# Queries and keys turned by VectorE blocks and a trip through DRAM instead of on TensorE, with plain float32 scores

## What is computed

```python
# layer 0: q, k turned by position (rope); layers 1 and 3: q, k normalised by their rms, times a weight
q = (layernorm(x) @ Wq).reshape(B, S, 32, 128);  k = (ctx @ Wk).reshape(B, S, 8, 128);  v = (ctx @ Wv)...
scores = einsum('bhqd,bhkd->bhqk', q, repeat(k, 4)) / sqrt(128) + mask
attn = softmax(scores);  x = x + tanh(g) * (einsum('bhqk,bhkd->bhqd', attn, v) @ Wo)
```

## Time and profile before

| | us |
|---|---|
| median of 3 runs | 2615.45 (2614.41 to 2617.41) |
| span of the profiled execution | 2614.6 |
| PE busy | 2382.5 (91%) |
| DVE busy | 1786.3 (68%) |
| POOL busy | 1512.2 (58%) |
| ACT busy | 1278.9 (49%) |

### The profile page before, as it was taken

How to read it: one execution, slowest core, us unless ns; L and a number is a source line. 1 busy time by engine, 2 the same in 40 slices (tenths; PEclk the granted TensorE clock), 3 DMA queues, 4 the chain that set the end, 5 groups by cost and what they waited for, 6 DMA issues and landing times.

```text
span 2614.6 us, 41410 instructions
## 1 busy us (share of the span) xinstructions
PE 2382.5 (91%) x13005; PEld 2016.6 (77%) x13005; DVE 1786.3 (68%) x3406; ACT 1278.9 (49%) x3698; POOL 1512.2 (58%) x1567
## 2 busy tenths in 40 slices
PE   5899999998889999999887887899689999999977
PEld 4788888886778888888766776776578888888753
DVE  4677777777877777777666676563477777777752
ACT  2555555554246666666534455233245666665421
POOL 5666666665246666666535667423456666666543
PEclk9999999999999999999999999899889999999979
DMA  3234444443224233223310000259513233322344
GB/s 110 80 118 155 141 160 159 151 162 109 71 84 142 97 98 102 93 93 98 109 49 17 1 1 27 81 193 365 175 61 108 91 98 101 101 94 77 116 169 151
DMA packets 191532, 288.12 MB, mean 110 GB/s; under 512 B 15985, under 2 KB 110833, under 8 KB 188378
## 3 DMA queue, kind: packets, MB, share of 16 engines
q1 hardware_dynamic: 175584, 236.34, 27.1%
q0 software_dynamic: 10224, 42.03, 4.6%
q10 hardware_dynamic: 5514, 7.11, 0.9%
HBM read 218.80 MB, written 100.37 MB: 122 GB/s over the span
## 4 chain that ended last, share of the span: by engine, by line
PE 73%; DVE 8%; DMA 6%; POOL 5%; issue 4%; ACT 3%; SPq 0%; POOLq 0%; ACTq 0%; DVEq 0%
PE B_qkv L806 32%; PE B_out L806 19%; PE B_more L883 4%; PE B_s L863 4%; PE B_qT L852 3%; DMA slots_y<-S 3%; PE B_more L806 2%; PE B_s L864 1%; PE B_more L957 1%; DMA out_x<-rows_last 1%; PE B_s L806 1%; DVE xn L1523 1%; DVE X L1650 1%; PE B_qT L806 1%; PE B_more L855 1%
## 5 line engine op out<-in xcount | busy, mean ns | idle before, releaser
L1333 ACT ACTIVATE W<-S,nmx 128x128 f32<-128x128 f32 x768 | 298.1, 395 | 49.9 <-DVE nmx L1625 48.8
L2183 POOL TENSOR_TENSOR S<-S,mask 128x512 f32<-128x512 f32 x184 | 256.6, 1394 | 46.9 <-ACT S L1162 46.9
L1226 ACT ACTIVATE sq<-B_qkv 128x640 f32<-128x640 f32 x127 | 89.7, 706 | 380.1 <-PE B_qkv L806 380.1
L2228 POOL TENSOR_TENSOR pT_l<-W,pT_h 128x512 fp32r<-128x512 f32 x184 | 241.8, 1314 | 32.9 <-ACT pT_h L1162 30.7
L2157 POOL TENSOR_SCALAR rn<-ss 128x5 f32<-128x5 f32 x128 | 25.3, 198 | 371.3 <-DVE ss L1563 371.3
L806 PE MATMUL B_qkv<-ring_h,xnT_h 128*128 128x512 f32 x540 | 216.2, 400 | 11.3 <-DVE spare_l L1474 4.8
L2222 POOL TENSOR_TENSOR W<-W,rden 128x512 f32<-128x512 f32 x192 | 202.1, 1052 | 32.7 <-DVE rden L1630 32.6
L806 PE MATMUL B_qkv<-ring_l,xnT_h 128*128 128x512 f32 x540 | 214.5, 397 | 0.0
L806 PE MATMUL B_out<-ring_h,oT_h 128*128 128x512 f32 x516 | 206.1, 399 | 8.7 <-DVE kT L1615 4.4
L806 PE MATMUL B_qkv<-ring_h,xnT_l 128*128 128x512 f32 x540 | 212.8, 394 | 0.0
L863 PE MATMUL B_s<-kT,qT_h 128*128 128x256 f32 x768 | 191.1, 326 | 17.8 <-DVE xnT_l L1474 15.1
(11 more groups left out here) (514 smaller groups left out, 7730.5 us busy)
## 6 DMA issues: line engine op xcount, KB each, us to landing
raw<-in_pieces SPq DMA_DIRECT2D x270, 256.0 KB, 2.6
between_p<-S SPq DMA_DIRECT2D x184, 256.0 KB, 2.2
W<-between_p SPq DMA_DIRECT2D x184, 256.0 KB, 2.8
slots_x<-in_zero SPq DMA_DIRECT2D x32, 1030.0 KB, 6.0
raw<-in_experts SPq DMA_DIRECT2D x16, 768.0 KB, 6.5
w<-in_experts SPq DMA_DIRECT2D x8, 1024.0 KB, 14.0
slots_y<-S SPq DMA_DIRECT2D x31, 256.0 KB, 6.4
xn<-slots_x ACTq DMA_DIRECT2D x8, 257.5 KB, 5.8
```

The costliest lines, as they stand in the source:

```text
L1333: t = act.activation(W[:, k, cols(r)], S[:, k, cols(r)], ACT.Exp, bias=nmx[:, k, r:r + 1], accum_out=den[:, k, r:r + 1])
L2183: pool.tensor_tensor(S3, S3, m.unsqueeze(1).to_broadcast([P, R, P]), ALU.add).then_inc(*masked.now((layer, u)))
L2228: pool.tensor_tensor(heads_first(pT[1][:, :]), by_block(W[:, k, :]), heads_first(f32(pT[0][:, :])), ALU.subtract).then_inc(*p_split.now((l ...
```

## The change

For all units but those of TURNED_BY_PE, q and k are turned as the probabilities are. Per such unit:

- PE no longer turns q and k (5 products with the identity), ACT and DVE no longer split them in high and low parts.
- `blocks_q` (i+1, 19 in the norm layers, 22 in the rope layer): DVE turns the 32x32 blocks of `qk` into `sq`, 640 columns. `store_q` (i+1, 63) writes `sq` to DRAM (320 KB), `load_q` (i+1, 64) reads it back into `qkT` in rows by block; it waits for the store to have landed and for the queries of the unit before to have been copied. `copy_k` (i+2, 30): ACT copies the keys (with their weight) and then the four heads of queries from `qkT` to rows packed by head, `keys` and `queries`.
- `scores` (i+2, 40): one plain float32 product of 128 columns for each head, into the single bank `B_sc`.
- `low_scores` goes, on ACT and POOL. `mask` on DVE scales the scores and adds the mask in one instruction.
- `sq` is free again when `store_q` has landed (`sq_read`). What writes it next, ACT's squares in the norm layers and DVE's product with cos in the rope layer, waits for that.
- Units with odd u in the middle of a layer project into the two banks `B_turn`, which the turned q and k had, and the others into `B_qkv`.

The units of TURNED_BY_PE still turn q and k on PE, and have the plain float32 scores too.

```diff
-            self.at(i + 1, 50, "turn_q", layer, u)
-            self.at(i + 1, 50, "split_k", layer, u)
+            if (layer, u) in TURNED_BY_PE:
+                self.at(i + 1, 50, "turn_q", layer, u)
+                self.at(i + 1, 50, "copy_k", layer, u)
+            else:
+                self.at(i + 1, 19 if KINDS[layer] == "norm" else 22, "blocks_q", layer, u)
+                self.at(i + 1, 63, "store_q", layer, u)
+                self.at(i + 1, 64, "load_q", layer, u)
+                self.at(i + 2, 30, "copy_k", layer, u)
             self.at(i + 2, 40, "scores", layer, u)
-            self.at(i + 2, 41, "low_scores", layer, u)
...
+            if NB <= u < G * NB - NB and u % 2:
+                return B_turn, ("qT", "kT")
+            return B_qkv, ("qkv",)
...
+        def sq_read(layer, u):
+
+            if (layer, u) in TURNED_BY_PE:
+                return (summed if KINDS[layer] == "norm" else roped).of((layer, u))
+            return q_stored[unit(layer, u)[3]].of((layer, u))
...
                 for r in range(R):
-                    pe.matmul(B_s[:, cols(r, 2 * P)], qT[0][:, cols(r)], kT_both[:, :], start=True, stop=False)
-                    t = pe.matmul(B_s[:, cols(2 * r)], qT[1][:, cols(r)], kT[0], start=False, stop=True)
+                    t = pe.matmul(B_sc[:, cols(r)], query(r), keys[:, :], start=True, stop=True)
...
+                    act.wait_ge(*q_loaded[unit(layer, u)[3]].of((layer, u)))
+                    copy(keys_by_block, keys_in, scale).then_inc(*keys_made.now((layer, u)))
+                    copy(queries[:, :, :], qkT[:, :, 0:R].rearrange("p t r -> p r t")).then_inc(*q_copied.now((layer, u)))
...
                     if u:
+                        dve.wait_ge(*sq_read(layer, u - 1))
                         dve.wait_ge(*roped.of((layer, u - 1)))
...
+            def blocks_q(layer, u):
+
+                kind = KINDS[layer]
+                dve.wait_ge(*{"rope": roped, "norm": normed}[kind].of((layer, u)))
+                if kind == "norm":
+                    dve.wait_ge(*summed.of((layer, u)))
+                dve.transpose(sq_blocks, qk[:, :].rearrange("p (h j q) -> p h j q", j=BLOCKS, q=BLOCK)
+                              ).then_inc(*q_blocks.now((layer, u)))
...
+                dve.scalar_tensor_tensor(out=S3, in0=per_head(B_sc), scalar=SCALE, in1=m.unsqueeze(1).to_broadcast([P, R, P]),
+                                         op0=ALU.mult, op1=ALU.add).then_inc(*sc_read.now((layer, u)))
...
+            def store_q(layer, u):
+                k = unit(layer, u)[3]
+                sync.wait_ge(*q_blocks.of((layer, u)))
+                if q_loaded[k].made:
+                    sync.wait_ge(q_loaded[k].sem, q_loaded[k].by * q_loaded[k].made)
+                sync.dma_start(between_q[k].rearrange("(p n) -> p n", p=P), sq[:, :]).then_inc(*q_stored[k].now((layer, u)))
+
+            def load_q(layer, u):
+                k = unit(layer, u)[3]
+                sync.wait_ge(*q_stored[k].of((layer, u)))
+                if u and (layer, u - 1) not in TURNED_BY_PE:
+                    sync.wait_ge(*q_copied.of((layer, u - 1)))
```

More of the change, by code:

```diff
@@ L465, in build @@
         sq = sb("sq", [P, (R + 1) * P])
+        with ExitStack() as besides_small_heads:
+            qkT = besides_small_heads.enter_context(nc.sbuf_tensor("qkT", [P, P, R + 1], F32))
+            keys = besides_small_heads.enter_context(nc.sbuf_tensor("keys", [P, P], F32))
+            queries = besides_small_heads.enter_context(nc.sbuf_tensor("queries", [P, R, P], F32))
         qT = [sb(f"qT_{k}", [P, HG], F32R) for k in "hl"]
@@ L629, in build @@
                                 "pT_hi", "oT_hi"))
-        rows_hi, low_scored = signal("rows_hi"), signal("low_scored")
+        rows_hi, keys_made, q_copied, q_blocks = (signal(n) for n in ("rows_hi", "keys_made", "q_copied", "q_blocks"))
+        q_stored, q_loaded = ([signal(f"{n}{k}", 16) for k in range(2)] for n in ("q_stored", "q_loaded"))
         y_copied = {"act": signal("y_copied_act"), "dve": signal("y_copied_dve")}
@@ L1312, in scores @@
                 qT_reader[:] = [scored.of((layer, u))]
-            def low_scores(layer, u):
-                k = unit(layer, u)[3]
-                act.wait_ge(*scored.of((layer, u)))
-                if layer == 0 and u == 0:
-                    act.wait_ge(*const.of("mask0"))
-                if layer == 3 and u < 2:
-                    for t in range(TILES2 - 2, TILES2):
-                        act.wait_ge(*y_stored[t % 2].of((2, t)))
-                elif k in S_reader:
-                    act.wait_ge(*S_reader[k])
-                copy(per_head(S[:, k, :]), score_parts[:, :, 1, :], SCALE).then_inc(*low_scored.now((layer, u)))
             def exp(layer, u):
@@ L1472, in vector_program @@
         def vector_program(dve):
+            S_reader = {}
             def sub(dst, a, b):
@@ L1588, in normalise @@
                 if u or layer == 1:
-                    dve.wait_ge(*qk_turned.of((layer, u - 1) if u else (0, len(plan.units[0]) - 1)))
+                    dve.wait_ge(*(qk_read(layer, u - 1) if u else qk_read(0, len(plan.units[0]) - 1)))
                 else:
@@ L1618, in mask @@
-            def mask(layer, u):
-                k = unit(layer, u)[3]
+            def blocks_q(layer, u):
[5 more added lines that the diff above has]
+                              ).then_inc(*q_blocks.now((layer, u)))
+            def mask(layer, u):
+                kind, g, b, k, vs = unit(layer, u)
+                dve.wait_ge(*scored.of((layer, u)))
+                if layer == 0 and u == 0:
+                    dve.wait_ge(*const.of("mask0"))
+                if layer == 1 and u == 0:
+                    dve.wait_ge(*small["mask13"].of(0))
+                if layer == 3 and u < 2:
+                    for t in range(TILES2 - 2, TILES2):
+                        dve.wait_ge(*y_stored[t % 2].of((2, t)))
+                elif k in S_reader:
+                    dve.wait_ge(*S_reader[k])
+                m = mask0[:, b, :] if kind == "rope" else mask13[:, :]
@@ L1624, in mask @@
+                S_reader[k] = (exped if (layer, u) in TURNED_BY_PE else p_stored[k]).of((layer, u))
                 dve.wait_ge(*sc_read.of((layer, u)))
-                dve.tensor_reduce(nmx[:, k, :], S3, AX, ALU.max, negate=True).then_inc(*maxed.now((layer, u)))
+                dve.tensor_reduce(nmx[:, k, :], per_head(S[:, k, :]), AX, ALU.max, negate=True).then_inc(*maxed.now((layer, u)))
             def denominators(layer, u):
@@ L2373, in load_p @@
                                between_p[k].rearrange("(i p n) -> p i n", i=BLOCKS, p=P)).then_inc(*p_loaded[k].now((layer, u)))
+            def store_q(layer, u):
[9 more added lines that the diff above has]
+                    sync.wait_ge(*q_copied.of((layer, u - 1)))
+                elif layer == 1:
+                    sync.wait_ge(*q_copied.of((0, len(plan.units[0]) - 1)))
+                elif layer == 3:
+                    sync.wait_ge(*scored.of(CHUNKS - 1))
+                    sync.wait_ge(*kbd_made2.of(NB - 1))
+                sync.dma_start(qkT[:, :, :].rearrange("p (i q) h -> p i (q h)", i=BLOCKS), between_q[k].rearrange("(i p n) -> p i n", i=BLOCKS, p=P)
+                               ).then_inc(*q_loaded[k].now((layer, u)))
             def fill_tables():
@@ L2413, in sync_program @@
                     parts[name](*args)
-            for done in (*landed, *p_stored, *p_loaded, scales_in, cols_in, cleared, *consts2_in, dispatch_in, *y_stored, *scattered, *rows_in, *weight_in, *x_in, *small.values(), *rope_in):
+            for done in (*landed, *p_stored, *p_loaded, *q_stored, *q_loaded, scales_in, cols_in, cleared, *consts2_in, dispatch_in, *y_stored, *scattered, *rows_in, *weight_in, *x_in, *small.values(), *rope_in):
                 if done.made:
```

129 lines of the change are left out of this document (51 added, 78 removed).

## The result

The changed kernel takes **3440.14 us** (median of 4 runs, 3432.38 to 3448.66), against 2616.43 for the kernel before (4 runs): ratio **1.3138**, interval 1.3107 to 1.3169. It is slower by 824 us. The forecast was 3216 with a range of 2950 to 3450: the sign and the mechanism hold, the size was 224 us short, and the measured time lies only 10 us under the upper end.

The account below looks back on a forecast made before the run. PE bounds the kernel before; after the change the loop through sq and q's store was to bind. Norm layers 417, rope layer 83, clearing stores 54 and edges 47 give +601 on 2614.6: 3216 us, range 2950 to 3450.

Parts of the forecast that it names:

- What bounds before, and PE's part: PE alone sets the pace in the steady middles; its work falls from 9.05 to about 8.6 us a unit.
- ACT ahead of the scores: Scores wait for ACT's oT_h, keys and queries: PE stands still some 1.7 us a unit, giving 10.3 us.
- The rival of 2845: If the loop through sq is shorter than 10.3 us, only ACT's standstill remains: +230, 2845 us; chance 0.12.
- The norm loop: Norm layers, squares through p's store and q's store to next squares: 13.1 us against 9.05; 103 x 4.05 = 417.
- PE fits in, with 2.9 us to spare: Norm layers: scores and projections end at 10.2 us, 2.9 before squares may start, so PE is not in the loop.
- The rope layer: DVE's product with cos writes sq and waits for q's store: 10.7 us a unit, 50 x 1.65 = 83.
- PE falls back in: Waits lower PE's clock; if over 2.9 us is lost, a norm unit costs about 1 us more: 3320; chance 0.16.
- The clearing stores: q's store stands behind a clearing store in the queue: +1.7 us in 32 steps, 54 us.
- The edges: 31 units at the edges of the layers, priced by no row: 1.5 us each taken, 47 us.
- the sum of 601: Norm layers 417, rope layer 83, clearing stores 54 and edges 47, added to the profiled 2614.6 us.

Follow-up runs that it names:

- Experiment 8: Against the kernel before: q and k of all units turned on PE, no DRAM trip, but plain float32 scores and DVE's mask; 2583.93 us, ratio 0.9867.
- Experiment 1: Changed kernel with q's store issued right behind DVE's turn of its blocks, ahead of the probabilities' load and its wait; 3065.79 us, ratio 1.1712.
- experiment 4: Changed kernel with q's store and load moved ahead of SP's wait for p's store, and key and query copies ahead of oT_h; 2833.29 us.
- experiment 2: Changed kernel with ACT's squares written to another buffer in units 8 to 39 of layer 1, so they need not wait for q's store; 3405.14 us.

## Why the prediction was right, and where its size was off

- **What bounds before, and PE's part.** Right. The turn of q is PE's only saving; the scores took 0.89 us where 0.92 was taken. Experiment 8's row gives 0.89 us, 0.02 more than the float32r products had. By the four passes of true float32 (the Trainium skill, FP8 and Floating Point Precision, TensorE Precision Notes) PE would have kept less of its 0.48 us; no cost of that kind shows in this row.
- **ACT ahead of the scores.** The order was right, two prices were not: queries took 1.12 us, not 0.60, keys 0.47 to 0.56, not 0.36. Experiment 1 shows the step by itself: PE stands still 2.15 us where 1.7 was worked out, and the unit is 10.93 us where 10.3 was. What the step left out is the clock: 19 of the 44 units ran below the full one, at 12.68 us. The rival of 2845 says this with the lower prices, and its nearest kernel is that of experiment 1 (3066). That experiment 4 came to 2833 does not bear it out, since there the copies stand first.
- **The norm loop.** Right in every link. The two turns from 1501.20 to 1528.89 average: squares to p's store 7.66 us (worked out 7.50; q's blocks were 1.34, not 0.80), the wait 2.41 (2.31), the issue 0.46 (0.38), q's landing 3.25 (2.8), the start 0.06 (0.1). That is 13.85 for 13.1. Over the steady stretches it is 13.79 and 13.74: 103 x (13.77 - 9.05) = 486 us, against 417. The largest part that was too small is q's landing.
- **PE fits in, with 2.9 us to spare.** It does, in the norm layers: PE's next work behind the projections starts at 1511.44, 2.5 us before the squares of 1513.93, and PE's clock hardly matters there: the 8 of 44 units at the full clock take 13.59 us, the 36 others 13.84. But it was weighed for one turn only. Followed over two units, the loop over q's load and the projections takes 13.0 us (experiment 2), only 0.8 behind the first.
- **The rope layer.** This is the term that was mis-sized: 10.7 us (its terms add up to 10.76), with the clears in 17 of 36 units 11.5, and measured 14.22. 50 x (14.22 - 9.05) = 258 us, against 83 + 54 = 137. The loop followed was the right one in 29 units of 37, but its links were too short. In the mean of the 36 units, from the product with cos to p's store it took 6.20 us, where 5.18 was read from one unit: 9 of the 36 did take 5.15 to 5.18, but 27 took 5.6 to 6.9, and in the rows looked at (at 309.81 and 399.19 us) the longer one has a low weight part on DVE and one on POOL ahead of p's blocks, which the shorter one has not. The prediction averaged these in the norm loop and left them out here. The wait took 2.66 (2.3), the issue 0.47 (0.38). Landing took 4.51 (2.8, and 0.8 for the clears): 3.33 without a clear, 5.82 with one. The last 0.38 (0.1) holds PE's share: in the 8 units that ended through PE the product with cos came 1.5 us after sq was free, 0.3 us over all units.
- **PE falls back in.** This rival's mechanism is there, in the 8 rope units of 37 in which PE came last; in the unit shown it did 4.26 us of work in 5.81 at the lower clock. In the norm layers it did not decide. PE's busy share came to 71% in layer 0 and 74% in layer 1, where 80 and 65 were given; the mean granted clock was 0.86 and 0.87, where the earlier trace rows has 1.00. That waits for data put the clock back in each turn of a loop is also what the Trainium skill tells (TensorE: Matmul & The Clock Gate, HAM oscillation); the trace agrees for most turns: 36 of 44 units of layer 1 had a mean clock under 1.00.
- **The clearing stores.** About right: 1.7 us was priced for each, and units with one took 2.15 us more than those without. The landing shown above (7.5 us where 4.5 was the row) was one of the long ones. Moving the stores to another queue gave back 16 us, not the 50 to 80 then expected, since they still ran beside p's store.
- **The edges.** What is left of 3430.2 - 2614.6 = 816 is 816 - 486 - 258 = 72 us, 2.3 for each of the 31 units, against 1.5. This is a remainder, not a measured stretch.

Together 69 + 121 + 25 = 215 us more than the sum of 601. That the range still held, by 10 us, owes something to luck: its bounds for a rope unit, 10.2 to 12.0 us and 1 to 3 for a clear, do not reach the 14.22 measured.

## What to carry to other kernels

A single queue with waits in it runs in order: before a new transfer goes in, list which wait of which other unit stands ahead of it; here three numbers in an order table held 607 of 824 us. A loop must be followed as far as it goes, over two units if a load is used one step later, and each price taken from a row of the same stride and from more than one unit: one without a weight part stood for all, and the rope term came out a us short. When the queue no longer binds, the engine behind it may run at its lower clock: price the work at both. A change of several parts is tried in parts: here the scores alone gave 1.3%, and the trip gained only in the norm layers, and only where its store, load and copies stood early and its rows were contiguous.

## What the hardware showed that was not expected

- A blockwise transpose of 128x640 on DVE took 1.34 us writing with a stride of five elements and 0.82 contiguous; ACT's copy of 128x512 took 1.12 us reading with that stride and 0.62 contiguous.
- Eight records of plain float32 took 1.05 us with 128 columns (experiment 8) and 1.06 with 8, both at the full clock: in these rows the columns were not what set their time.
- In experiment 1 the granted clock fell to the lower level in 19 of 44 norm units, and in 13 of these PE had stood still only 2.1 us ahead of the scores. They took 12.5 us; units at the full clock, behind the same standstill, took 10.9.
- Taking 1030 KB stores off SP's queue made one store land 1.4 us sooner and another 1.0 us later, in the median, with the same bytes to move.
